# Last node block of a fused edge loop: its TensorE and ScalarE steps placed in front of and between the last two sort groups

## The reference, cut to what matters

```python
msg_in = jnp.concatenate([nodes[senders], edges], axis=-1)
agg = jax.ops.segment_sum(msg_in @ W_message, receivers, num_segments=total_nodes)
h = _layer_norm(jax.nn.relu(agg) + nodes, ln_aggr_scale, ln_aggr_bias)
nodes_out = _relu_mlp_skip(h, [W0, W1, W2], [b0, b1, b2])
x = _layernorm(x + _layer_norm(nodes + nodes_out, ln_out_scale, ln_out_bias))
```

## Time and profile before

| | before |
|---|---|
| median of 3 runs (lowest to highest) | 5342.7 us (5336.64 to 5343.07) |
| the profiled execution, its own time | 5340.55 us |
| its span (first to last instruction) | 5338.8 us |
| PE busy | 3915.3 us, 73% |
| POOL busy | 3607.4 us, 68% |
| DVE busy | 3517.3 us, 66% |
| ACT busy | 1876.9 us, 35% |

### The profile page before, as it was taken

How to read it: one execution, slowest core, us unless ns; L and a number is a source line. 1 busy time by engine, 2 the same in 40 slices (tenths; PEclk the granted TensorE clock), 3 DMA queues, 4 the chain that set the end, 5 groups by cost and what they waited for, 6 DMA issues and landing times. The chain is left out here.

```text
span 5338.8 us, 86704 instructions
## 1 busy us (share of the span) xinstructions
PE 3915.3 (73%) x18660; PEld 3020.1 (57%) x18661; DVE 3517.3 (66%) x11286; ACT 1876.9 (35%) x5324; POOL 3607.4 (68%) x3655
## 2 busy tenths in 40 slices
PE   4488989898989898989898366666666666666661
PEld 3366666666666666666665255555555555555551
DVE  8777777777777777777776455555555555555554
ACT  0133333333333333333332043333333333333334
POOL 0377776767776767677764177777777777777772
PEclk9799999999999999999998688888888888888886
DMA  1356555555555555555556244444444444444443
GB/s 44 98 161 166 158 159 154 160 153 159 156 160 154 159 154 159 153 158 155 160 153 115 85 107 106 106 106 106 106 106 106 106 106 106 106 106 106 106 105 64
DMA packets 544286, 679.76 MB, mean 127 GB/s; under 512 B 340246, under 2 KB 376430, under 8 KB 543996
## 3 DMA queue, kind: packets, MB, share of 16 engines
q0 software_dynamic: 174144, 469.02, 32.9%
q1 hardware_dynamic: 355132, 196.63, 14.3%
q10 hardware_dynamic: 14976, 13.69, 0.7%
HBM read 650.32 MB, written 27.79 MB: 127 GB/s over the span
## 5 line engine op out<-in xcount | busy, mean ns | idle before, releaser
L615 POOL DMA_INDIRECT rows<-in_x,picked x1785 | 1798.0, 1007 | 745.2 <-issue 591.3
L1459 POOL DMA_INDIRECT room<-nodetab,nbr_idx x1736 | 1643.5, 947 | 562.4 <-issue 492.0
L663 PE MATMUL bank<-rows,hot 128*128 128x320 f32 x3570 | 1271.6, 457 | 7.8 <-DMA rows<-in_edge 4.8
L648 PE MATMUL bank<-w_edge,feats 128*128 128x258 f32 x3264 | 1032.3, 407 | 324.3 <-ACT bank L783 312.1
L1489 PE MATMUL bank<-room,w 128*128 128x258 f32 x3472 | 1049.8, 466 | 53.2 <-ACT w L1535 52.7
L1521 ACT ACTIVATE w<-off,logit 128x128 f32<-128x128 bf16 x1736 | 534.0, 388 | 1357.8 <-DVE logit L1573 1357.8
L1489 PEld LDWEIGHTS bank<-room,w 128*128 128x128 f32 x3472 | 811.7, 241 | 249.4 <-ACT w L1535 96.3
L648 PEld LDWEIGHTS bank<-w_edge,feats 128*128 128x128 f32 x3264 | 588.2, 200 | 521.7 <-ACT bank L783 364.8
L1480 PE MATMUL bank<-ident,w 128*128 128x128 f32 x1736 | 309.1, 331 | 761.4 <-ACT w L1521 761.4
L783 ACT COPY bank<-b_edge 128x258 f32<-128x258 f32 x1634 | 601.2, 377 | 656.4 <-DVE unused L1002 595.0
L663 PEld LDWEIGHTS bank<-rows,hot 128*128 128x128 f32 x3570 | 721.7, 202 | 173.1 <-issue 38.5
(11 more groups left out here) (313 smaller groups left out, 4085.8 us busy)
## 6 DMA issues: line engine op xcount, KB each, us to landing
feats<-in_edge SPq DMA_DIRECT2D x408, 256.0 KB, 2.9
rows<-in_edge SPq DMA_DIRECT2D x255, 128.0 KB, 3.1
rows<-in_x,picked POOLq DMA_INDIRECT x1785, 2.8
room<-nodetab,nbr_idx POOLq DMA_INDIRECT x1736
rows<-in_edge SPq DMA_DIRECT2D x153, 160.0 KB, 3.3
nodetab<-tab ACTq DMA_DIRECT2D x52, 129.0 KB, 3.1
x_blk<-in_x SPq DMA_DIRECT2D x52, 128.0 KB, 2.0
x_rows<-u_n ACTq DMA_DIRECT2D x52, 128.0 KB
```

Of the source, the lines that this page charges most:

```text
L615: pool.indirect_dma_start(out=rows[:, STARTS[j] + s, 0:D], out_offset=None, in_=a["x"], in_offset=bass.IndirectOffsetOnAxis(ap=picked[j][: ...
L648: mm(y, feats[:, f0 * P:(f0 + 1) * P], w_edge[:], start=False, stop=True, skip_group_check=True).then_inc(o["y_ready"], 1)
L663: ins = mm(S_PS, hot[j % HR][:, s - STARTS[j], :], rows[:, s, :], start=(s == 0), stop=(s == SA - 1), skip_group_check=True)
L1459: pool.indirect_dma_start(out=nbr[:, u * GC + k, :], out_offset=None, in_=nodetab, in_offset=bass.IndirectOffsetOnAxis(ap=nbr_idx[u][:, k: ...
```

## The change: what it does

It rewrites the straight code behind the loop on two engines. In the new text PE does `turn_s` and `messages` of block `n` ahead of sort group 0, `turn_h0` between `sort` and `turn_rows` of group 0, the first `layer` ahead of sort group 1, and the second between `sort` and `turn_rows` of group 1; the other steps follow. ACT's list is interleaved the same way: `take_s` and the first `deviation`, `pack` 0, `take_h0`, `keep_rows` 0, the first `layer`, `pack` 1, the second `layer`, `keep_rows` 1, then the rest. DVE, POOL and SP keep their lists, and so does the loop. No instruction is added or dropped.

```diff
@@ PE, behind the loop
-                for u in range(U):
-                    sort(n, u, tuple(range(L)))
-                    turn_rows(n, u)
-                for kk in sorted(node):
-                    node[kk](n)
+                steps = [node[kk] for kk in sorted(node)]
+                steps[0](n)
+                steps[1](n)
+                sort(n, 0, tuple(range(L)))
+                steps[2](n)
+                turn_rows(n, 0)
+                steps[3](n)
+                sort(n, 1, tuple(range(L)))
+                steps[4](n)
+                turn_rows(n, 1)
+                for step in steps[5:]:
+                    step(n)
@@ ACT, behind the loop
-                for u in range(U):
-                    pack(n, u)
-                    keep_rows(n, u)
-                for kk in sorted(node):
-                    node[kk](n)
+                steps = [node[kk] for kk in sorted(node)]
+                steps[0](n)
+                steps[1](n)
+                pack(n, 0)
+                steps[2](n)
+                keep_rows(n, 0)
+                steps[3](n)
+                pack(n, 1)
+                steps[4](n)
+                keep_rows(n, 1)
+                for step in steps[5:]:
+                    step(n)
```

## The result

| | before | after |
|---|---|---|
| median of 13 runs each (lowest to highest) | 5339.64 us (5336.64 to 5343.07) | 5327.85 us (5321.81 to 5331.31) |
| ratio, 95% interval | | 0.9976 [0.9968, 0.9985] |
| span of the profiled execution | 5338.8 us | 5322.1 us |
| PE busy | 3915.3 us | 3887.8 us |

The medians are 11.8 us apart, 0.22% of the time before. The ratio in the table, 0.24% less, is not the quotient of the two medians; its interval says 8.0 to 17.1 us (0.0015 and 0.0032 of 5339.64). The change is faster, clear of no change.

A forecast was written before the change was run, and what follows sets the result against it. The chain of hand-offs behind the loop bounds that stretch, PE's clock second. Between 14.7 us won (early clock rise) and 11.8 (later), 13.7 was taken: 5342.7 - 13.7 = 5329.0 us, range 5325 to 5336.5.

The forecast's parts named there:

- Start of the node block: Behind the loop: turn_s at 2944.45, ACT out of the loop after 0.79 us, messages' result there between 2947.9 and 2949.5.
- The rival of a late exit: PE or ACT comes out of the loop late; at the upper bound 4.3 us won, 5338.4 us; chance 0.10.
- `add_x`: DVE's first node step starts at the last tag's end, about 2949.45 instead of 2962.49, 13.0 us earlier.
- Group 0: First sort group, ahead of turn_h0: costs the chain 1.15 us at half clock, nothing at full.
- the early case: PE's full clock returns within the first sort group; layer 2 starts 13.4 us sooner, 14.7 us won in all.
- Group 1: Second sort group, between layers 0 and 1: gives back 2.6 us at half clock or 1.5 at full.
- Behind layer 2: Full clock shortens layer 2 by 1.0 us and back by 0.3.
- The rival of a clock that stays at half: PE's clock stays at half past layer 1: 9.2 us won, 5333.5 us; chance 0.20.
- The chain is not what ends the stage: POOL's last write or SP's wait ends the stage, so nothing is won, 5342.7 us; chance 0.03.
- the gain lies elsewhere: Rival stated with a follow-up run: the gain lies outside the stretch from the last s_cur to the next stage.
- Slower through late rows: The second sort group's rows reach POOL's last write too late to end the stage in time: some 5358 us; chance 0.02.
- that sign of being wrong: The prediction is wrong if the loop of layer 1 takes a different time; no size given.

The follow-up runs named there:

- e1: Kernel before with only turn_s, messages (PE) and take_s (ACT) moved ahead of both sort groups; 6850.97 against 6859.74 us, ratio 0.9981.
- a2: Changed kernel without edit, third profile, on one chip with the kernel before; 5334.22 us, ratio 0.9977.
- e5: Changed kernel plus 16 matmuls that nothing reads, 4 behind turn_s and 12 behind messages; 6680.37 against 6692.1 us, ratio 0.9981.
- e10: Changed kernel with the sort in pieces in PE's gaps, its end mended, plus 16 matmuls that nothing reads; 6680.69 us, ratio 0.9972.
- e8: Changed kernel with sort group 1, its turn_rows and ACT's copies for it moved ahead of layer 0; 5334.62 us, ratio 0.9978.
- b2: Kernel before, unchanged, profiled a second time; 5347.96 us, ratio to its own twin 1.0001.
- e2: Changed kernel with sort group 1 moved behind back on PE and its ACT copies later; 6850.14 us, ratio 0.998.
- e3: Changed kernel with both sort groups cut in pieces laid in PE's gaps, ACT's copies moved to suit; 6828.19 us, ratio 0.9959.
- e11: Changed kernel with the sort in pieces in PE's gaps, group 1's turn_rows ahead of turn_x1 and ACT copies earlier, rerun; 5331.01 against 5347.28 us, ratio 0.9972.
- a1: Changed kernel again without edit, with its own profile; 6845.54 against 6859.74 us, ratio 0.9976.
- e9: Changed kernel with the sort in pieces in PE's gaps, group 1's turn_rows ahead of turn_x1 and ACT copies earlier, first run; 6681.05 us, ratio 0.9973.
- e6: Kernel before, order kept, plus 36 matmuls that nothing reads ahead of sort group 0; 6693.4 against 6692.1 us, ratio 0.9999.

## Why the prediction was right, point by point

| W, us | profiles |
|---|---|
| before | 47.58, 45.91 |
| changed | 32.96, 32.34, 32.71 |

**The forecast.** The sum was 13.7 us, 5329.0 us and 0.26%. Measured were 0.24% in the first comparison (5327.85 us) and 0.23% in the second (13.1 us). By the means of the profiles' W (46.75 and 32.67) it is 14.1 us. The prediction was right in its mechanism and its verdict, and its sum was close; the parts were less exact than the sum, and some luck was in it. The forecast time of 5329.0 us started from a median of three runs, 5342.7, which over 13 runs is 5339.64; the gain between the medians is 11.8 us, so the time is met to 1.2 us and the gain to 1.9.

**Start of the node block.** `turn_s` 0.05 us behind `s_cur`, as forecast; `messages` ended under the tags (at 2946.05; the tags ended at 2947.63). The 0.79 us for ACT's way out of the loop was too much: ACT had its last loop instruction end at 2943.04 and started `take_s` at 2943.49, right behind `turn_s`, so 0.45 is an upper bound. It cost nothing, since DVE was the later one. The rival of a late exit didn't occur.

**`add_x`.** From 18.6 us behind `s_cur` to 5.4: 13.2 us sooner; forecast 13.0. e1 shows that this start by itself is worth only 4 us, as long as the sort stays ahead of the rest.

**Group 0.** Forecast: back 1.15 us at half clock, 0.45 in the early case. Measured: the whole group ran at half clock (4.18 us) in the profile after and in a2, and e5 shows 1.2 us for it. The early case's term was mis-sized, since it let the clock return within the group; it came back when the group ended, here at about 2952. The Trainium skill ("TensorE: Matmul & The Clock Gate", section on the HAM clock gate) makes the point of return differ from run to run; the five profiles of the two kernels agree, with the second group of before once at 3.76 and once at 2.23 us.

**Group 1.** Forecast: back 1.5 us at full clock. Measured: layer 1 started 2955.97 - 2954.08 = 1.89 us behind layer 0's end, against 1.18 without a group between, so 0.7. I had priced 16 matmuls at 4 x 0.68 from the loop's groups of four. Such rows don't add up: at full clock 2 of these matmuls take 0.42 us and 3 take 0.55 (e10), 13 take 1.83 (e10) and 16 take 2.22, so by these rows each costs 0.13 us and a row 0.16 once. That this error (0.8 us) and the one of group 0 (0.7 us) nearly cancel is luck: layer 2 started 13.4 us sooner in relation to `s_cur`, which is the forecast of the early case to a tenth.

**Behind layer 2.** Forecast 1.3 us (layer 2 and `back` at full clock). From layer 2's start to the next stage it was 18.3 us and is 2975.26 - 2958.19 = 17.07: 1.2.

**The rival of a clock that stays at half** asked for 9.2 us. In none of the three profiles of the changed kernel did the layers run at half. Its sum took the second group at 3.76 us as half clock; that group ended with the clock already back, and one wholly at half takes 4.18, so it should have read 8.8.

**Order and clock.** The gain isn't the order's alone. From before to after, the three layers take 2.9 us less, group 1 takes 1.5 less and `back` 0.25 less, all through the granted clock. As an estimate from these rows, about 4.7 of the 14.6 us come from the clock that the denser order brought back, and about 9.9 from the order itself. No run has the changed kernel's order with the clock at half in all the layers, so this split is not shown by an experiment.

**The chain is not what ends the stage, or the gain lies elsewhere:** the first is refuted by W, which follows the chain in e1, e5 and e8. The second is settled by cutting the spans at `s_cur` and at the next stage's first instruction. Of the 16.7 us between the profiles before and after, 1.6 lie ahead of that `s_cur`, 14.6 in W and 0.5 behind it; of the 17.8 us between b2 and a2, 3.1, 13.2 and 1.5. All that follows the stretch, the loop of layer 1 included, takes 2346.8 to 2348.9 us in all four, so that sign of being wrong did not appear.

**Slower through late rows:** the mechanism is real, but from an earlier point than worked out. I said that POOL's last write decides the end only from a few us ahead of it; e2 and e3 put the price at 7.9 us from the write's start to the next stage. In the changed kernel the write starts 16.6 us ahead, so 8 to 9 us of slack are left.

**What stays open.** Between executions of one kernel the loops move more than the change does: from the first to the last `s_cur` it is 2679.0 and 2689.3 us in the two profiles of before and 2679.3 and 2687.1 in two of the changed kernel. That is the scatter which the interval of 9 us shows. Whether the gap kernel (e11) is faster than the changed kernel was not settled: its W is 1.8 us less and its median 3.2 us less, and the intervals of the two overlap for the most part.

## What to carry to other kernels

A tail of dependent steps behind a loop is worth reading by each engine's written order: ask for each step when its input was ready and what stood ahead of it, on all the engines of the chain, and lay independent work where the chain is on another engine. Moving the start alone brought 4 us of 14 here, and a single 0.3 us instruction left behind the bulk work on a second engine held back 2 more. The independent work must not slide too far back either, if its result has a DMA to go before a barrier: here that path needed 7.9 us.

## What the runs showed that I had not expected

The same program took 5340 us in one comparison, 5347 in another, and 6692 and 6860 us in two others, for the kernel before and all variants alike. In the profile of the changed kernel at 6845 us the fused loop took 3664 us from the first to the last `s_cur` instead of 2679, with the same instructions and bytes. Windows from the middle of the loop, of the changed kernel in the profile after and in a1:

```profile
1000.00:2900.00 1900.00, 1661.80 (x7658) 1240.62 (x7657) 1464.26 (x5094) 676.10 (x1872) 1330.80 (x1312) 0.94 0.57 155
```

```profile
1000.00:3000.00 2000.00, 1458.37 (x5900) 1039.58 (x5898) 1135.13 (x3900) 515.76 (x1433) 1005.62 (x1006) 0.84 0.41 113
```

Every engine is busy for a smaller share and the granted clock is lower. The duration of single DVE instructions is as before (the row of `s_cur` 0.55 us in both); TensorE's are longer with the lower clock (the `edge` matmuls 447 ns in the mean against 407), which does not account for the difference: over the whole loop PE is busy 2683 us against 2349. And the stretch behind the loop takes the same 32 to 33 us. So what is longer is for the most part waits inside the loops. The trace of a1 ascribes part of them to "remote" (454.8 us ahead of the DVE instruction of the logits), a releaser that doesn't appear among the larger waits at the usual time. Its cause stays open.

Extra matmuls that nothing reads seem to bring TensorE's full clock back sooner. In both profiles that have 16 of them in the new order the clock was back ahead of group 0 or early in it: in e5 the group took 2.23 us instead of 3.79 to 4.18, in e10 its first 11 tiles took 1.86 instead of 2.93 (e9, e11). Of the profiles without them only e3 had it full there, left over from the loop. Two profiles are few, and in e6, with 36 of them and 2.8 us of idle time behind, the clock fell within the group.
